# First attention to the context: scores once, by query, with four heads side by side

## The reference

```python
q = k = v = ...          # q: x by heads; k and v: the same context by heads
scores = einsum('bhqd,bhkd->bhqk', q, k) * 32 ** -0.5
scores = where(k_index > q_index, -inf, scores)
m = scores.max(-1); p = exp(scores - m)
out = einsum('bhqk,bhkd->bhqd', p / p.sum(-1), v)
x = layernorm(x + out)
```

## Time and profile before

| | |
|---|---|
| median of 3 runs | 2840.01 us (2838.26 to 2840.66) |
| profiled execution, its own time | 2836.32 us |
| its span in the profile | 2834.5 us |
| mean granted clock of PE | 0.901 |
| busy share of the span: PE, weight loads | 85%, 66% |
| busy share of the span: DVE, ACT, POOL | 44%, 30%, 25% |
| PE's clock in slices 13 to 16 of 40 | 9, 7, 8, 9 tenths of full speed |

### The profile page before, as it was taken

The page is one execution under the profiler, slowest core; times in us unless marked ns, Lnnn a source line. Parts: engine busy times, 40 slices in busy tenths (PEclk is TensorE's granted clock), DMA queues, the critical chain, the costliest instruction groups (busy, mean ns, idle before and its releaser), DMA issues. The chain is left out here.

```text
span 2834.5 us, 37569 instructions
## 1 busy us (share of the span) xinstructions
PE 2405.4 (85%) x14496; PEld 1879.0 (66%) x14496; DVE 1236.4 (44%) x2784; ACT 855.3 (30%) x1295; POOL 709.5 (25%) x667
## 2 busy tenths in 40 slices
PE   6999999999975888789999996678777855999974
PEld 4989889889864666678887775555453644555542
DVE  2343443343454553531111233465555455567535
ACT  2222222222222434322111112344444222444332
POOL 2532332231302532024333001433332010121210
PEclk8999999999986978899999998797788976999986
DMA  4000000000006652101000000321220645534101
GB/s 175 20 8 12 27 19 9 12 19 9 1 1 135 130 107 55 49 30 53 15 30 0 1 1 27 53 45 32 40 47 16 212 119 110 120 89 94 44 8 60
DMA packets 91967, 144.10 MB, mean 51 GB/s; under 512 B 10864, under 2 KB 64752, under 8 KB 88816
## 3 DMA queue, kind: packets, MB, share of 16 engines
q1 hardware_dynamic: 91792, 141.71, 20.5%
HBM read 82.95 MB, written 17.30 MB: 35 GB/s over the span
## 5 line engine op out<-in xcount | busy, mean ns | idle before, releaser
L1183 PE MATMUL PS<-WH,bXH 128*128 128x512 f32 x512 | 201.6, 394 | 5.4 <-POOL WL L1460 5.4
L1183 PE MATMUL PS<-WL,bXH 128*128 128x512 f32 x512 | 200.8, 392 | 0.0
L1183 PE MATMUL PS<-WH,bXL 128*128 128x512 f32 x512 | 200.8, 392 | 0.0
L558 DVE TENSOR_TENSOR xN<-PS,xN 128x512 f32<-128x512 f32 x128 | 88.5, 692 | 227.7 <-PE PS L361 227.7
L1852 DVE TENSOR_REDUCE aM<-PS 128x4 f32<-128x1024 f32 x128 | 153.1, 1219 | 67.0 <-PE PS L1694 66.3
L1378 DVE SCALAR_TENSOR_TENSOR s<-s,cf,PS 128x256 f32<-128x256 f32 x112 | 53.9, 481 | 250.2 <-ACT s L1298 241.2
L330 PE MATMUL PS<-aXH,QKH 128*128 128x512 f32 x384 | 152.3, 397 | 0.0
L330 PE MATMUL PS<-aXH,QKL 128*128 128x512 f32 x384 | 149.6, 390 | 0.0
L330 PE MATMUL PS<-aXL,QKH 128*128 128x512 f32 x384 | 149.6, 389 | 0.0
L1798 ACT ACTIVATE aPT<-PS 128x1024 f32<-128x1024 f32 x128 | 128.7, 1025 | 68.2 <-PE PS L1714 67.7
L643 POOL TENSOR_TENSOR E<-E,DM 128x256 f32<-128x256 f32 x64 | 47.1, 736 | 392.5 <-ACT E L475 392.5
(11 more groups left out here) (429 smaller groups left out, 6383.6 us busy)
## 6 DMA issues: line engine op xcount, KB each, us to landing
ckr<-in_cS SPq DMA_DIRECT2D x48, 256.0 KB, 7.1
cqs<-cQH SPq DMA_DIRECT2D x64, 128.0 KB, 3.8
sg<-in_gu SPq DMA_DIRECT2D x8, 1024.0 KB, 5.0
aqs<-aQH SPq DMA_DIRECT2D x64, 128.0 KB, 4.0
xks<-zkH SPq DMA_DIRECT2D x16, 512.0 KB, 8.2
xqs<-xQH SPq DMA_DIRECT2D x64, 128.0 KB, 2.6
gQK<-in_Wqk SPq DMA_DIRECT2D x8, 768.0 KB, 4.3
V<-in_xT SPq DMA_DIRECT2D x4, 1024.0 KB, 6.0
```

Source lines behind the costliest of these rows:

```text
L558: e.tensor_tensor(xN[:, t, :], PS[:, b, :], xN[:, t, :], ALU.add).then_inc(o_add.sem, 1)
L1183: mm = e.matmul(PS[:, b, :], x[:, kc, 128 * t:128 * t + 128], w[:, kc, :], start=kc == 0 and i == 0, stop=kc == KC - 1 and i == 2)
```

## The change

Scores are made once, with the queries in the partitions, for a group of four heads at a time. The four lie in four sets of 32 partitions of `QH`/`QL` (queries, scaled by minus 32 to the power -0.5) and `KH`/`KL` (keys), as the turns leave them, so nothing is restacked; each head writes a bank of its own, 0 to 3, which are held for that throughout. Queries 0 to 127 take only keys 0 to 127. DVE adds the bar in place and takes the minimum of the negated scores (`tensor_tensor_reduce`); ACT takes exp(-scores + minimum) with that minimum as bias and has the sums of the exps as `accum_out`; PE turns the exps (**flip**, two heads at a time, three transposes a head); ACT and DVE copy half the groups each to `PT`; then come the values, without the columns of ones. The quotient is taken tile by tile, with the sums from ACT. Gone are the second scores, the bar's matmuls, the turn of the maxima and their way over HBM, the restacking, and the memsets of ones. The keys come in one transfer per block, already turned, and POOL splits them.

The order, one slot after another and by the second number within one:

```diff
+    at = {}
+    def put(slot, order, what, j, i=0):
+        at.setdefault(slot, []).append((order, len(at), (what, j, i)))
+    for j in range(J):
+        base = 8 * j
+        put(base - 8, 3, "context", j)
+        put(base - 6, 5, "turn", j)
+        for g in range(4):
+            put(base + 2 * g - 1, 9, "scores", j, g)
+            put(base + 2 * g, 1, "soft", j, 2 * g)
+            put(base + 2 * g + 1, 1, "soft", j, 2 * g + 1)
+            put(base + 2 * g + 1, 2, "flip", j, 2 * g)
+            put(base + 2 * g + 2, 2, "flip", j, 2 * g + 1)
+            put(base + 2 * g + 3, 6, "pv", j, g)
+        put(base + 11, 8, "fin", j, 0)
+        put(base + 12, 8, "fin", j, 1)
+        if j % 2 and j < 7:
+            for i, what in enumerate(("n1", "n2", "n3", "n4")):
+                put(base + 15 + i, 8, what, j)
+    plan = [what for slot in sorted(at) for _, _, what in sorted(at[slot], key=lambda x: x[:2])]
```

On PE (`y` is j % 2; `n` counts groups):

```diff
+    spans = ((0, 128), (128, 384))
...
+                n = 4 * j + i
                 if i == 0:
+                    e.wait_ge(*k_lo.upto(j + 1))
+                    e.wait_ge(*q_lo.upto(j + 1))
+                if n:
+                    e.wait_ge(*s_exp.upto(2 * n))
+                for q in (0, 1):
+                    a, b = spans[q]
+                    for k, (w, x) in enumerate(pair3((QH[y], KH[y]), (QL[y], KL[y]))):
+                        for r in range(4):
+                            mm = e.matmul(PS[:, r, a:b], w[32 * r:32 * r + 32, i, 128 * q:128 * q + 128],
+                                          x[32 * r:32 * r + 32, i, 0:b - a], start=q == 0 and k == 0, stop=k == 2,
+                                          skip_group_check=True)
+                mm.then_inc(s_in.sem, 1)
+            elif what == "flip":
+                b, left = rooms["flip", j, i]
+                for w in left:
+                    e.wait_ge(*w)
+                e.wait_ge(*s_exp.upto(8 * j + i + 1))
                 for a in (0, 1):
+                    for c in range(3):
+                        mm = e.transpose(PS[:, b + a, 128 * c:128 * c + 128],
+                                         P[(i // 2) % 2][:, 2 * (i % 2) + a, c, :], idF[:, :])
+                mm.then_inc(f_in.sem, 1)
+            elif what == "pv":
+                b, left = rooms["pv", j, i]
+                for w in left:
+                    e.wait_ge(*w)
+                e.wait_ge(*flipped(8 * j + 2 * i))
+                e.wait_ge(*flipped(8 * j + 2 * i + 1))
+                e.wait_ge(*in_v[j % 3].upto(j // 3 + 1))
+                for kt in (0, 1):
+                    for r in range(4):
+                        h = 4 * i + r
+                        mm = e.matmul(PS[32 * r:32 * r + 32, b, 128 * kt:256], V[j % 3][:, kt, 32 * h:32 * h + 32],
+                                      PT[i % 2][:, r, 256 * kt:256 + 128 * kt], start=kt == 0, stop=True,
...
+                mm.then_inc(a_mm.sem, 1)
...
+                b, left = rooms["fin", j, i]
+                for w in left:
+                    e.wait_ge(*w)
+                e.wait_ge(*a_out.upto(4 * j + 4))
+                for g in range(4):
+                    mm = e.transpose(PS[:, b, 128 * g:128 * g + 128], nT[y][:, g, 128 * i:128 * i + 128], idF[:, :])
+                mm.then_inc(n_mm.sem, 1)
```

On ACT:

```diff
+            if what == "turn":
...
+                if j >= 2:
+                    e.wait_ge(*s_in.upto(4 * j - 4))
+                e.wait_ge(*x_mm.upto(j + 1))
+                e.activation(QH[y][:, :, :], PS[:, b:b + 2, :].rearrange("p k (a n) -> p (k a) n", a=2), ACTF.Copy,
+                             scale=-SC).then_inc(q_hi.sem, 1)
+            elif what == "soft":
                 n = 8 * j + i
+                if n >= 4 and n % 2 == 0:
+                    e.wait_ge(*f_in.upto(n - 2))
+                if j >= 2 and i == 0:
+                    e.wait_ge(*n_rec.upto(j - 1))
+                for a in (0, 1):
+                    h, r = 2 * i + a, 2 * (i % 2) + a
+                    e.wait_ge(*s_max.upto(2 * n + a + 1))
+                    e.activation(P[(i // 2) % 2][:, r, 0, :], PS[:, r, 0:128], ACTF.Exp, bias=M[y][:, 0, h:h + 1],
+                                 scale=-1.0, accum_out=den[y][:, 0, h, :])
+                    last = e.activation(P[(i // 2) % 2][:, r, 1:3, :].rearrange("p c k -> p (c k)"), PS[:, r, 128:384],
+                                        ACTF.Exp, bias=M[y][:, 1, h:h + 1], scale=-1.0, accum_out=den[y][:, 1, h, :])
+                last.then_inc(s_exp.sem, 1)
+            elif what == "flip" and i % 2 == 0:
+                n = 8 * j + i
+                b = rooms["flip", j, i][0]
+                if n >= 4:
+                    e.wait_ge(*a_mm.upto((n - 4) // 2 + 1))
+                e.wait_ge(*f_in.upto(n + 1))
+                e.activation(PT[(i // 2) % 2][:, 0:2, :], PS[:, b:b + 2, 0:384], ACTF.Copy).then_inc(f_act.sem, 1)
             elif what == "pv":
+                if j >= 2:
+                    e.wait_ge(*n_mm.upto(2 * j - 2))
+                e.wait_ge(*a_mm.upto(4 * j + i + 1))
+                e.activation(nT[y][:, i, :], PS[:, rooms["pv", j, i][0], 0:256], ACTF.Copy).then_inc(a_out.sem, 1)
```

On DVE:

```diff
+            if what == "turn":
                 b = rooms["turn", j][0]
+                if j >= 2:
+                    e.wait_ge(*s_in.upto(4 * j - 4))
                 e.wait_ge(*q_hi.upto(j + 1))
+                for k in (0, 1):
+                    last = e.scalar_tensor_tensor(out=QL[y][:, 2 * k:2 * k + 2, :].rearrange("p a n -> p (a n)"),
+                                                  in0=PS[:, b + k, :], scalar=-SC,
+                                                  in1=QH[y][:, 2 * k:2 * k + 2, :].rearrange("p a n -> p (a n)").bitcast(F32),
+                                                  op0=ALU.mult, op1=ALU.subtract)
+                last.then_inc(q_lo.sem, 1)
+            elif what == "soft":
+                if j == 0 and i == 0:
+                    e.wait_ge(*bars.upto(1))
+                if j >= 2 and i == 0:
+                    e.wait_ge(*s_exp.upto(8 * j - 8))
+                e.wait_ge(*s_in.upto(4 * j + i // 2 + 1))
+                for a in (0, 1):
+                    h, r = 2 * i + a, 2 * (i % 2) + a
+                    for q in (0, 1):
+                        lo, hi = spans[q]
+                        s = PS[:, r, lo:hi]
+                        last = e.tensor_tensor_reduce(out=s, in0=s, in1=BAR[:, 256 - 128 * q:384],
+                                                      scale=1.0, scalar=3.0e38, op0=ALU.add, op1=ALU.min,
+                                                      accum_out=M[y][:, q, h:h + 1])
+                    last.then_inc(s_max.sem, 1)
+            elif what == "flip" and i % 2:
+                n = 8 * j + i
+                b = rooms["flip", j, i][0]
+                if n >= 4:
+                    e.wait_ge(*a_mm.upto((n - 4) // 2 + 1))
+                e.wait_ge(*f_in.upto(n + 1))
+                e.tensor_copy(PT[(i // 2) % 2][:, 2:4, :], PS[:, b:b + 2, 0:384]).then_inc(f_dve.sem, 1)
+            elif what == "fin":
+                if i == 0:
+                    e.wait_ge(*s_exp.upto(8 * j + 8))
+                    if j:
+                        e.wait_ge(*n_out.upto(2 * j))
+                    e.reciprocal(rc[:, :, :, :], den[y][:, :, :, :]).then_inc(n_rec.sem, 1)
+                    e.wait_ge(*n_rec.upto(j + 1))
...
+                    e.wait_ge(*added.upto(2 * j - 1 + i))
+                e.wait_ge(*n_mm.upto(2 * j + i + 1))
+                e.tensor_tensor(oN[:, i, :].rearrange("p (h c) -> p h c", h=16),
+                                PS[:, rooms["fin", j, i][0], :].rearrange("p (h c) -> p h c", h=16),
+                                rc[:, i, :, :].broadcast_to([128, 16, 32]), ALU.mult).then_inc(n_out.sem, 1)
```

On POOL, and on SP:

```diff
+            if what == "context":
+                if j >= 2:
+                    e.wait_ge(*s_in.upto(4 * j - 4))
+                e.wait_ge(*in_c[y].upto(j // 2 + 1))
+                e.tensor_copy(KH[y][:, :, :], cst[y][:, :, :]).then_inc(k_hi.sem, 1)
+                e.wait_ge(*k_hi.upto(j + 1))
+                e.tensor_tensor(KL[y][:, :, :], cst[y][:, :, :], KH[y][:, :, :].bitcast(F32),
                                 ALU.subtract).then_inc(k_lo.sem, 1)
...
+        for j in (0, 1):
+            e.dma_start(cst[j][:, :, :], d["cT"][:, :, 256 * j:256 * j + 256]).then_inc(in_c[j].sem, 16)
+            e.dma_start(V[j][:, :, :], d["c"][:, 2 * j:2 * j + 2, :]).then_inc(in_v[j].sem, 16)
+        for j in range(2, J):
+            e.wait_ge(*k_lo.upto(j - 1))
+            e.dma_start(cst[j % 2][:, :, :], d["cT"][:, :, 256 * j:256 * j + 256]).then_inc(in_c[j % 2].sem, 16)
+            if j >= 3:
+                e.wait_ge(*a_mm.upto(4 * j - 8))
+            e.dma_start(V[j % 3][:, :, :], d["c"][:, 2 * j:2 * j + 2, :]).then_inc(in_v[j % 3].sem, 16)
```

(17 more changed lines are left out.)

318 lines of the change are left out of this document (51 added, 267 removed).

## The result

The changed kernel took 2804.69 us (median of four runs, 2800.65 to 2809.15), the kernel before 2840.34: a ratio of 0.9875 with a 95% interval of 0.9858 to 0.9893, some 36 us faster. Forecast were 2808 us. The profiled execution took 2809.15 us, its span is 2807.4.

What follows compares the result with a forecast made beforehand. The prediction took a PE-DVE-ACT ring, passed 32 times, to bound the changed loop. Loop -19, head -12.8 and tail -0.8 made about -32 us: 2836.3 - 32 + 3.7 = 2808 us, range 2774 to 2846.

Steps and rivals of the forecast that it cites:

- the loop: First scores to end of the last exp: 198 + 37 = 235 us against 254.3, so -19.
- The ring: Attention loop: PE, DVE and ACT wait on each other in 32 turns of 6.2 us, 198 us.
- Clock: PE's mean granted clock in the loop taken as 0.65, three turns in ten at the full clock.
- Cold throughout: Rival for the loop: PE holds every turn at 6.5 us, +10 and extras +2, 2820 us; chance 0.25.
- warm and cheap: Rival for the loop: all at 2.4 GHz, 5.55 us a turn or 5.13 without sums, 2774 to 2787; chance 0.2.
- Scores: PE's 24 score matmuls, four heads side by side: 0.48 us at 2.4 GHz, 0.96 at 1.2.
- a sign of being wrong: Scores on PE: the forecast is wrong if the 24 score matmuls take over 1.5 us.
- Exps: ACT's two exps per head: 0.69 us plus 0.1 for each sum, 0.9 a head, ends 0.69 and 1.03.
- Interruptions: Added to the ring: next queries' turn 15 us, second quotient with its transposes 7, three layer norms 15.
- Head: Before the first scores: transfers gone and norm earlier, scores at 864.4 instead of 877.24, -12.8 us.
- Tail: Last exp to the next stage's first matmul: about 8.5 us for 9.3, -0.8, within the error.
- The rule on transposes: PE's clock: transposes don't raise it as other matmuls do, so the ring, half transposes, would stay cold.

Runs made afterwards that it cites:

- e8: Changed kernel with scores issued two heads at a time and DVE's copy of a turned half behind the next pair's bars: 2841.2 us, ratio 0.9989.
- e11: Changed kernel with scores two heads at a time, transposes ahead of the next scores, first queries copied ahead of the norm's apply: 2821.8 us, ratio 0.9942.
- e10: Changed kernel with 12 unread 128x128 bf16 matmuls on PE ahead of each group's first turn: 2795.3 us, ratio 0.9853.
- e2: Changed kernel with only the high times high product of the scores, 8 matmuls for 24: 2793.8 us, one run.
- e3: Changed kernel with the same 24 score matmuls issued head by head instead of four heads in turn: 2851.4 us, one run.
- e7: Changed kernel with two heads at a time, DVE's copy and queries' part late, first queries ahead of the norm's apply: 2787.9 us, ratio 0.9806.
- e4: Changed kernel with the next queries' turn moved behind the third group's scores and the second quotient one step later: 2814.8 us, one run.

## Why the prediction was right

The mechanism was right and the sum was right, but the sum partly by luck: several of its terms were wrong by 3 us and more, and they cancelled. The stage is shorter by 32.1 us, as forecast; the loop gave 4 us more than its -19, the head 3.5 less than its -12.8.

- **The ring.** Right: 32 turns, PE waiting for the exps, no transfer, ACT ending last at the full clock and PE at the low. Turns at the full clock took 5.64 to 5.74 us for the forecast 5.55. The turn at the low clock was priced too low: 7.28 and 7.41 for 6.5. Heads 0 and 1 were done after 4.40 and not 3.83, six transposes took 1.44 and not 1.2 (the 0.23 each that the prediction read in the earlier trace rows make 1.4), the values 1.44 and not 1.29. The mean of the seven turns that nothing interrupts was 6.32 for 6.2, since the low clock was rarer than assumed.
- **Clock.** 0.79 in the loop for 0.65: 58% of its time was passed at 2.4 GHz, not three tenths. With 7.3 for the low turn, a clock of 0.65 would have made a turn of 6.9 us, some 20 us more in the loop than the 198 of the sum; that the two errors cancelled is luck. "Cold throughout" and "warm and cheap" both fell.
- **Scores.** Side by side, as taken, but dearer: 0.89 us to the transposes at 2.4 GHz and 1.59 at 1.2, DVE beginning after 1.01 and 1.70, for 0.84 and 1.3. At the low clock that is past the 1.5 us which the prediction named as a sign of being wrong. The step that failed is counting columns; the row shows sets of four at one pace.
- **Exps.** A head 0.80 us, forecast 0.9. The sum was nearly right (0.08 to 0.09 for 0.1), the exps without it take 0.63 and not 0.69. At the full clock this made up for the scores. ACT was busy 152.5 us in the stage for "some 175", DVE 163.4 for 160.
- **Interruptions.** Queries with the first quotient 8.88 - 6.32, seven times, 18 us (15); the third turn of a block, which in all but the first block holds the second quotient, 6.71 - 6.32, eight times, 3 (7); what is left, three norms above all, some 9 (15). These differences hold what the clock did in those turns as well. With 32 x 6.32 = 202 less the 0.8 by which the last turn is short: 231, for 235.
- **Head.** A miss, -9.3 for -12.8: the norm was not freed. The holds by the keys' split, priced in the loop, were left out here.
- **Tail.** +0.3 for -0.8, within the error given.
- **The rule on transposes.** In the changed kernel the clock was granted in full even in a stretch with little work: 1.00 from 964 to 972, with PE busy 2.67 of 8 us (the row is below). So the rule's strong form, a ring that stays cold, did not come true. In the denser orders it nearly did: 0.63 in e8 and 0.67 in e11. The prediction's row for it is weak: its sixteen transposes at 0.50 began after 4.54 us in which PE waited, so a cold start explains them as well. The Trainium skill (TensorE: Matmul & The Clock Gate, Part 4: PE-mode transpose) says that transposes do not count as PE work for the clock in the way that other matmuls do. e10, where 384 plain matmuls took it from 0.79 to 0.95 at about the same busy share, agrees, but does not show it. That transposes rather than the 32-row scores hold it down was not tried by itself; e2, with a third of the scores, was granted 0.76, and e3, with the same matmuls in another order, 0.65, one execution each.

The stretch view of the changed kernel from 964 to 972:

```profile
964.00:972.00 8.00, 2.67 (x36) 1.72 (x34) 6.09 (x17) 4.10 (x16) 0.41 (x1) 1.00 0.25 90
```

What stays open is what the clock follows here, and so whether an order exists that is as dense as e7's and runs at 2.4 GHz.

## What to carry to other kernels

Where one set of banks goes round through three engines, price the turn, not the engines: nearly all that a link saves arrives (0.08 to 0.09 us in each of 256 exps gave 17 us, 17.8 us of scores gave 16.5), and whatever stands in a queue between two links is paid as well. Before moving an interruption, follow its banks as well as its queue: in e4 and e8 a wait taken from one engine came back on another. And a denser queue on PE wasn't a faster one where it ran at 1.2 GHz (e8, e11): look at the granted clock of the stretch before believing an order. A forecast that comes out right can still hold wrong terms that cancel: check each term against its row, and not the sum alone.

## What the runs showed that I had not expected

- Sets of four 32-row matmuls start 0.11 to 0.17 us apart at 2.4 GHz, with 128 columns as with 256 (0.21 to 0.32 at 1.2 GHz).
- Reading ACT's sums is an instruction of its own (0.19 to 0.21 us in the rows), half covered by the exp beside it.
- PE without a gap stayed at 1.2 GHz for 15 us (e8), and had 2.4 GHz in the emptiest stretch of the changed loop.
- The same head took 11.1 to 16.1 us from kernel to kernel without an edit to it: the keys came at another point of the norm's chain, and POOL held one of its operations in e3 (0.89 us) and four in e8 (1.04, 2.20, 0.95 and 2.19).
